# Cross-attention of a two-layer Perceiver block: scores, context block and query products in another order, and the last two experts' rows of the first tile added by TensorE

## The reference

```python
x = x + _L0_xattn_ref(_layernorm(x), ctx_1024, ctx_1024, mask, ...)   # cross-attention, masked, 16 heads of 64
x = x + _L0_attn_ref(_layernorm(x), ...)                              # gated self-attention
x = x + _L0_ffn_ref(_layernorm(x), ...)                               # 64 experts, top 8, capacity 128
x = x + _L1_xattn_ref(_layernorm(x), ctx_1024, ctx_1024, ...)         # cross-attention, 16 heads of 64
x = x + _L1_attn_ref(_layernorm(x), ...)
x = x + _L1_ffn_ref(_layernorm(x), ...)                               # 8 experts, top 2
```

```python
q = (Q @ Wq.T + bq); k = (K @ Wk.T + bk); v = (V @ Wv.T + bv)
scores = einsum('nqhd,nkhd->nqkh', q, k) / sqrt(64)
out = einsum('nqkh,nkhd->nqhd', softmax(scores, axis=2), v).reshape(n, lq, H * D) @ Wo.T + bo
```

## Time and profile before

| | |
|---|---|
| median of 3 runs | 2289.22 us (2286.27 to 2293.53) |
| profiled execution, own time | 2283.12 us |
| its span | 2281.3 us, mean granted TensorE clock 0.973 |
| TensorE matmul busy | 2170.7 us (95%) |
| VectorE busy | 1116.2 us (49%) |
| ScalarE busy | 330.8 us (15%) |
| GpSimd busy | 255.9 us (11%) |
| DMA queue of SyncE | 284.12 MB |

### The profile page before, as it was taken

How to read it: one execution, slowest core, us unless ns; L and a number is a source line. 1 busy time by engine, 2 the same in 40 slices (tenths; PEclk the granted TensorE clock), 3 DMA queues, 4 the chain that set the end, 5 groups by cost and what they waited for, 6 DMA issues and landing times. The chain is left out here.

```text
span 2281.3 us, 48070 instructions
## 1 busy us (share of the span) xinstructions
PE 2170.7 (95%) x19023; PEld 1624.5 (71%) x19023; DVE 1116.2 (49%) x2940; ACT 330.8 (15%) x775; POOL 255.9 (11%) x298
## 2 busy tenths in 40 slices
PE   7999999999889999999996999999999999899798
PEld 6788878888668888888874676666765766556443
DVE  3665433434444444444433556565565555466623
ACT  0000011111111111111111122212121221112110
POOL 0000000000034334434420000000000000001102
PEclk9999999999889999999997999999999999999799
DMA  7234420000259999999994312313313215400134
GB/s 261 91 99 155 118 89 11 19 9 9 92 184 333 330 331 327 335 328 331 329 341 155 125 60 75 110 38 120 101 42 124 78 65 165 176 12 29 47 125 152
DMA packets 93504, 337.64 MB, mean 148 GB/s; under 512 B 16016, under 2 KB 16784, under 8 KB 84065
## 3 DMA queue, kind: packets, MB, share of 16 engines
q1 hardware_dynamic: 65312, 284.12, 34.8%
q0 software_dynamic: 16576, 39.50, 6.8%
q10 hardware_dynamic: 11520, 12.65, 1.8%
HBM read 286.39 MB, written 51.25 MB: 148 GB/s over the span
## 5 line engine op out<-in xcount | busy, mean ns | idle before, releaser
L628 PEld LDWEIGHTS psum<-work,arena 128*128 128x128 f32 x3072 | 355.2, 193 | 31.7 <-issue 30.8
L628 PE MATMUL psum<-work,arena 128*128 128x128 f32 x3072 | 355.8, 276 | 1.4 <-ACT work L1736 1.4
L392 PEld LDWEIGHTS psum<-work,arena 128*128 128x128 f32 x2560 | 293.4, 194 | 8.9 <-issue 8.4
L392 PE MATMUL psum<-work,arena 128*128 128x128 f32 x2560 | 294.8, 278 | 3.8 <-DMA arena<-in_q 2.6
L1868 POOL TENSOR_TENSOR small<-small 128x1 f32<-128x1 f32 x136 | 72.4, 532 | 1963.7 <-issue 892.5
L704 PE MATMUL psum<-work,arena 128*128 128x257 f32 x1024 | 234.4, 382 | 0.7 <-DVE arena L1378 0.7
L1611 ACT COPY work<-psum 128x512 f32<-128x512 f32 (+1 forms) x182 | 97.0, 547 | 799.0 <-PE psum L303 719.7
L704 PEld LDWEIGHTS psum<-work,arena 128*128 128x128 f32 x1024 | 190.8, 191 | 28.1 <-issue 1.2
L398 PE MATMUL psum<-arena,work 128*128 128x512 f32 x448 | 204.6, 609 | 0.7 <-ACT work L1611 0.7
L636 PE MATMUL psum<-arena,work 128*128 128x512 f32 x384 | 182.0, 610 | 2.0 <-DVE work L1329 2.0
L726 PE MATMUL psum<-work 128*128 128x512 f32 x384 | 169.2, 593 | 0.0
(11 more groups left out here) (214 smaller groups left out, 2274.9 us busy)
## 6 DMA issues: line engine op xcount, KB each, us to landing
arena<-in_experts SPq DMA_DIRECT2D x64, 2304.0 KB, 9.1
expert_rows<-work SPq DMA_DIRECT2D x8, 2304.0 KB, 10.8
work<-in_ctxT SPq DMA_DIRECT2D x32, 514.0 KB, 4.9
work<-in_ctx SPq DMA_DIRECT2D x32, 512.0 KB, 4.3
work<-in_ctx_tail SPq DMA_DIRECT2D x32, 450.0 KB, 3.5
work<-last_key_probs ACTq DMA_DIRECT2D x32, 256.0 KB, 4.3
arena<-in_experts SPq DMA_DIRECT2D x8, 1024.0 KB, 15.5
arena<-in_qkv SPq DMA_DIRECT2D x1, 6144.0 KB, 19.3
```

The lines of the kernel that those rows point to most:

```text
L392: done = nc.tensor.matmul(to[:, n * P:(n + 1) * P], w[:, j, at:at + P], src[:, j * P:(j + 1) * P], start=(j == 0), stop=(j == KD - 1))
L628: done = nc.tensor.matmul(to[:, n * P:(n + 1) * P], w[:, at:at + P], xgT[e % 2][:, j * P:(j + 1) * P], start=(j == 0), stop=(j == KD - 1))
```

## The change

It has four parts, all in the written order of the streams.

1. In a tile's first sequence TensorE runs two row blocks of `scores(1)` before it turns any weights of sequence 0, a third between the two groups of transposes, and the fourth behind them. Since the banks still hold the scores of sequence 0, each of the first two blocks waits for ScalarE's exponential of that block (`s_e`).
2. In `mix_last` the last chunk (`j = 3`) comes behind `project_q` of the next tile. VectorE takes it behind `take_q`; SyncE's count for the load that waits for this chunk grows by 2.
3. For the last two experts VectorE builds a matrix `onehotT` that marks which slot belongs to which row of tile 0, and sends the rows of tile 0 out of bounds for their scatters. TensorE multiplies it with `y` and sums both experts in one PSUM bank; VectorE adds that to tile 0. SyncE reads tile 0 back after 62 scatters; the loads of biases stand ahead of it, the context loads still come behind scatter 64.
4. In the last round VectorE runs `silu_up` of expert 63 before `take_down` of expert 62.

```diff
+LATE = 2
+        onehotT = list(carve(work, 9216, *[CAP] * LATE))
@@ experts_pe
             eight(EXPERTS // ROUND - 1, True)
+            pe.wait_ge(s_onehotT, LATE)
+            for n in range(LATE):
+                pe.wait_ge(s_y_ready, EXPERTS - LATE + n + 1)
+                done = nc.tensor.matmul(bank[4], onehotT[n], y[n], start=(n == 0), stop=(n == LATE - 1))
+            done.then_inc(s_late, 1)
@@ cross_pe
-            def turn_q():
+            def turn_q(behind=0):
                 for half_ in range(2):
-                    wait(pe, s_proj_free, c.proj.value(1 - half_))
+                    wait(pe, s_proj_free, c.proj.value(behind + 1 - half_))
...
-            def scores(b, rows=range(4)):
+            def scores(b, rows=range(4), early=False):
...
                 for rt in rows:
+                    if early:
+                        wait(pe, s_e, c.e.value(3 - rt))
...
-            def mix_last(turned):
+            def mix_last(turned, between):
...
                 for j in range(2, KD):
+                    if j == KD - 1:
+                        between()
...
             def tile(final):
                 for b in range(SEQS - 1):
-                    turn_weights(lambda: scores(b + 1, range(0, 1)))
+                    c.e.add(4)
+                    if b == 0:
+                        scores(1, range(0, 2), True)
+                        turn_weights(lambda: scores(1, range(2, 3)))
+                    else:
+                        turn_weights(lambda: scores(b + 1, range(0, 1)))
                     turned = c.tp.value()
-                    scores(b + 1, range(1, 4))
+                    scores(b + 1, range(3 if b == 0 else 1, 4))
                     mix(b, turned)
+                c.e.add(4)
                 turn_weights(lambda: None if final else pe_turn_xn(pe, c, 1))
-                mix_last((c.tp.value(1), c.tp.value()))
+                mix_last((c.tp.value(1), c.tp.value()), lambda: None if final else project_q(KD - 1))
                 mixed = c.proj.value()
                 if not final:
-                    project_q(KD)
-                    turn_q()
+                    turn_q(1)
                     queries_wk()
@@ experts_dve, answer
+                if late:
+                    nc.vector.tensor_tensor(fidx, fidx, empty, ALU.add)
+                    dve.drain()
+                    nc.vector.tensor_scalar(onehotT[n % LATE], iota128, fidx, None, ALU.is_equal).then_inc(s_onehotT, 1)
+                    nc.vector.tensor_scalar(empty, fidx, float(P), float(NOWHERE), ALU.is_lt, ALU.mult)
+                    dve.drain()
@@ experts_dve, eight
-                    silu_up(e, r)
+                    if not (final and e == ROUND - 1):
+                        silu_up(e, r)
                     if not (final and e >= ROUND - 4):
                         ask(e + 4, r)
-                        answer(e + 4, r)
+                        answer(e + 4, r, final and e + 4 >= ROUND - LATE)
+                    if final and e == ROUND - 2:
+                        silu_up(e + 1, r)
                     take_down(e, r)
@@ cross_dve
-                take_mix(b, i, (3,))
...
                 take_last_mix(i)
                 if not final:
                     take_q()
+                take_mix(SEQS - 1, i, (KD - 1,))
+                if not final:
                     take_queries()
...
             dve.wait_ge(s_x_back[0], 16)
+            dve.wait_ge(s_late, 1)
+            nc.vector.tensor_tensor(x[:, 0:D], x[:, 0:D], bank[4], ALU.add)
             layernorm(dve, 0)
@@ sync
             load(wv1, "v1", KD, s_w["v1"])
-            sp.wait_ge(s_scatter, 16 * EXPERTS)
-            sp.dma_start(x[:, 0:D], x_d[0:P, :]).then_inc(s_x_back[0], 16)
             load_row(bq1, "bq1", s_w["bias_q1"])
...
+            sp.wait_ge(s_scatter, 16 * (EXPERTS - LATE))
+            sp.dma_start(x[:, 0:D], x_d[0:P, :]).then_inc(s_x_back[0], 16)
+            sp.wait_ge(s_late, 1)
+            sp.wait_ge(s_scatter, 16 * EXPERTS)
...
-            mixed = [KD, 2 * KD, 3 * KD, 4 * KD + 1]
+            mixed = [KD, 2 * KD, 3 * KD, 4 * KD + 3]
```

More of the change, by code:

```diff
@@ L254, in build @@
         s_scatter = sem("scattered")
+        s_onehotT, s_late = sem("late_onehot_ready"), sem("late_rows_full")
         s_ctxT = [sem("ctx_columns_even"), sem("ctx_columns_odd")]
@@ L802, in tile @@
                 project_out()
+            c.e.add(TILES * (2 + 1))
             for name in ("q1", "k1", "v1"):
@@ L813, in cross_pe @@
             pe.wait_ge(s_w["o1"], 16)
-            with rounds(pe, TILES - 1, [(c.xn, 1), (c.proj, CROSS_TILE), (c.tp, CROSS_TP), (c.p, 4 * SEQS),
+            with rounds(pe, TILES - 1, [(c.xn, 1), (c.proj, CROSS_TILE), (c.tp, CROSS_TP), (c.p, 4 * SEQS), (c.e, 4 * SEQS),
                                         *[(n, 16 * SEQS // 2) for n in c.ctxT + c.ctxr]]):
@@ L1306, in ask, with answer @@
                                         place.broadcast_to([P, TILES, CAP]), ALU.is_equal).then_inc(s_onehot, 1)
-            def answer(e, r):
+            def answer(e, r, late=False):
                 n = e % ROUND
```

## The result

The kernel after the change took 2278.11 us (median of 11 runs, 2270.76 to 2283.29), the kernel before 2290.44 us (11 runs, 2286.27 to 2298.88): a ratio of 0.9936, with a 95% interval of 0.9925 to 0.9948. By the ratio that is 14.7 us faster, 12 to 17 by its interval; the two medians lie 12.3 us apart. The forecast was 2273.9 us in a range of 2268 to 2281.

What follows compares the result with a forecast made beforehand. TensorE was taken as full in the fourth sublayer's loop, leaving waits at its start and a short pause per tile. Gains 9.9 + 3.5 + 1.9 = 15.3 us from the median 2289.22 gave 2273.9 us, range 2268 to 2281.

Steps and rivals of the forecast that it cites:

- The start of tile 0: End of the experts: TensorE starts tile 0 at 1208.2 instead of 1218.11, 9.9 us earlier (bounds 8.3 and 10.5).
- the landing of scatter 61: End of the experts: taken as 1199.8 us, when the read of tile 0 is issued; `take_down(63)` also waits for it.
- The read in the queue: SyncE's queue: tile 0's read, issued at 1199.8, stands behind four loads and lands at 1203.1; alone it takes 2.7 us.
- Sequence 0 of tile 0: Scores of sequence 1 first: TensorE's pause shrinks from 4.55 to 1.6 us; 3.5 us gained, bounds 5.2 and 1.9.
- the lower clock that was assumed behind the pause of 1.6 us: Tile 0's first sequence: a fall of the clock after the wait for the first exponential, costing TensorE 1.7 us.
- rival 2: Clock stays up more after pauses of 1.6 and 6 us: 19.3 us gained in all, 2269.9 us; chance 0.08.
- the pause of 6 us: Before tile 0: the remaining TensorE pause is again followed by the lower clock; loss of about 3.2 us left unchanged.
- The queries: Query products, 7 times: last chunk covers L1362, pause falls from 1.53 to 1.26 us; 0.27 each, 1.9 us in all.
- Sequence 0 in the loop: Loop tiles: new order removes no wait but issues the spread load later; costed at 0, at worst 2.4 us.
- rival 3: Sequence 0's spread load becomes the wait in 8 tiles: 3.0 us each, 24 us in all, 2298 us; chance 0.04.
- The cover of 0.2 us: Loop tiles: spread load lands at 1535.75, that much before VectorE begins the first chunk at 1535.97.
- the profiled execution would take 2267.8 us: Whole kernel: the profiled execution of 2283.12 us, less the 15.3 us gain.

Runs made afterwards that it cites:

- the end alone: Parts 3 and 4 alone put into the kernel before, with the cross-attention stream in its old order: 2278.36 us, ratio 0.9963 (0.9949 to 0.9976).

## Why the forecast was right

- *The start of tile 0* was forecast with its right cause and 1.4 us too much. `down(63)` ended at 1198.7 and TensorE then waited for `take_down(63)`, as said. L318 started at 1209.48 and not 1208.2, and the step that was too early is the landing of scatter 61. Forecast at 1199.8, it came at 1201.48: it was issued 0.9 us later than in the first profile of before, and landed 8.1 us behind its issue instead of 7.1 (GpSimd goes on 0.1 us behind that landing). In the five profiles with both parts 3 and 4 or part 3 alone, and the loads ahead of the read, it took 7.9 to 8.1 us; in the six of the old order 6.3 to 7.9, two of them 7.8 and 7.9; and with the loads behind the read 7.3 and 8.0. So it isn't shown that the change made this scatter slower: the forecast took its landing from one profile, in which it was early. What makes it vary stays open. From the addition to L318 it was 5.3 us against 5.1.
- *The read in the queue.* The forecast let it land 3.3 us after its issue; it took 2.7. Three of the four loads were gone by 1201.6, about as reckoned, but the read came later than reckoned and met an almost empty queue. That the queue matters is seen where the read came earlier. In the end alone the loads landed at 1191.5 to 1193.2 and the read, issued at 1189.78, took 3.8 us, to 1193.6. Without part 4 they landed at 1193.9 to 1195.6 and the read, issued at 1192.10, took 3.9. In both it landed 0.4 us behind the last of them. This agrees with what the Trainium skill, "DMA: Bandwidth & Descriptors", section "Queues, rings and completion order", states: on each DMA engine one ring's descriptors are consumed in order. That the read also landed last is what these runs show; the rule speaks of consuming, not of landing. With none of the four loads ahead the same read took 2.5 and 2.6.
- *Sequence 0 of tile 0* gained 5.4 us where 3.5 were forecast. The failed step is the lower clock that was assumed behind the pause of 1.6 us, from that behind a pause of 1.3 us at 291 us. The pause is there, 1.59 us; the granted clock is 1.00 before, in and behind it, and no fall followed in any of the nine profiles with this order. The row that the forecast went by was no rule either: the pause of 1.34 us at L457 is in all 14 profiles, and the lower level followed it in seven and not in the other seven. The same changed kernel has it both ways, first profile and third (windows just behind the pause, columns as above):

```profile
293.00:296.30 3.30, 3.30 (x10) 2.59 (x9) 0.00 (x0) 0.00 (x0) 0.00 (x0) 0.50 0.00 0
```

```profile
293.60:296.90 3.30, 3.30 (x17) 2.89 (x17) 0.27 (x1) 0.00 (x0) 0.00 (x0) 1.00 0.00 0
```

  So one profile couldn't tell what a pause costs. The gain of 5.4 us is the size that rival 2 gave (5.2), for this place alone; the lower level was there behind the pause of 6 us, as the forecast had it. It lasted until 4.7 to 7.7 us behind TensorE's start in the profiles of the old order and until 5.1 to 8.0 in those of the new, so leaving that term as it was did no harm.
- *The queries* gained 0.16 us a tile, not 0.27, 1.1 us in all. From the first `turn_q` to L699 it took 1.37 us instead of 1.26. ScalarE's first copy starts 0.64 us behind `turn_q`, as reckoned; with its 0.58 us it ends at 1481.30, and TensorE starts 0.15 us behind that, where I had put 0.05.
- *Sequence 0 in the loop*, costed at nothing, cost 0.2 to 0.4 us. The spread load is issued later, and in this tile the first chunk is met as before. The place in the changed kernel:

```profile
1423.87 0.60 PE L306 MATMUL psum<-ident,work 128*128 128x128 f32 x4
...
1426.82 0.35 ACTq L1817 DMA_DIRECT2D work<-last_key_probs  x1
```

```profile
1430.28 1.14 DVE L1436 SCALAR_TENSOR_TENSOR arena<-work,psum 128x512 f32<-128x512 f32 x1 [0.96 <-PE psum L736]
```

  Here VectorE waits 0.96 us for TensorE and not for the load, as before. But in five of the eight tiles of this profile the load came last, by 0.1 to 0.2 us: in tile 0 (the row at 1249.28 above), and most in this one:

```profile
1699.84 7.18 PE L736 MATMUL psum<-work 128*128 128x512 f32 x16
...
1702.13 1.14 DVE L1436 SCALAR_TENSOR_TENSOR arena<-work,psum 128x512 f32<-128x512 f32 x1 [1.19 <-DMA work<-last_key_probs]
```

  The product with the context took 7.18 us there instead of 7.03. Over the eight tiles such stretching makes 0.4 us, and 0.2 to 0.4 in the three profiles of the changed kernel. The load took 3.1 to 3.4 us, where rival 3 needed 5.5. The cover of 0.2 us was used up, and rival 3 came only as this trace of it.
- *Luck in the sum.* The stretches make 15.0 us where 15.3 were forecast, but term by term they are 1.4 and 0.8 too small and 1.9 too large: the agreement within 0.3 us comes from errors that cancel. The waits that each term named were right; the clock behind the pause of 1.6 us was not.
- *What was wrong:* the sentence that the profiled execution would take 2267.8 us. It took 2278.28, since the profile of before that the sum was taken from had a fifth sublayer that no other execution showed. The forecast of the time held because it went by the median of the runs.

## What to carry to other kernels

Read a gain from a stretch between two events, in several profiles, and the total from the medians: one profile of each kernel gave 4.8 us here, where the ratios of three comparisons over several runs gave 12.4, 14.2 and 14.7. In a wait that happens once, look for the serial step behind it; two small matmuls replaced the wait for two scatters and gave 8.5 us, while taking out a wait beside that step (part 4) gave nothing. Where an order has no slack, a moved load has to be counted to the tenth of a microsecond before it moves. What a pause does to the clock, too, is read from several profiles.

## What was not expected of the hardware

- In the middle of the fifth sublayer three bursts of 128 tiny matmuls took 1.9 to 2.0 us each, in one piece, in one execution, and such bursts mostly 3.8 to 4.1 us in the 13 others, in pieces with pauses for `issue`.
- Waits that are long met cost TensorE 0.06 and 0.08 us for each instruction that they made (125 in 7.4 us, 249 in 20).
- A load issued behind four large ones, before any of them had landed, held SyncE for 12.9 to 15.9 us; all that is queued behind it on that engine starts later.
- A pause of 1.59 us was followed by the lower clock in none of nine profiles, one of 1.34 us elsewhere in the same program in seven of 14, and for one and the same kernel in some executions and not in others. What tells them apart is open.
